# Group norm's inverse deviation: one power on Pool in place of ScalarE's square root and VectorE's reciprocal

## The chip, the cores and the metric

The kernel runs on one core of one Trainium2 chip. The metric is the device time of one execution in microseconds (us); lower is better. The engines of the core are named as the profile names them: PE is TensorE, DVE is VectorE, ACT is ScalarE, POOL is GpSimd, and SP issues the DMAs. Each works through its own list of instructions in order, and they wait for each other by semaphores.

## What is computed

Two layers run over a batch of 8, with 112 tokens of 512 channels each. The first is an RWKV-6 block: layer norm, five mixed inputs, a recurrence over the tokens for 32 heads of 16 channels, a group norm over each head, a gate, the output projection `Wo`, a second layer norm and a gated feed-forward part. The second layer lets its output attend to 375 context tokens, followed by an RMS norm and a feed-forward net. The part that the change touches is the group norm:

```python
y = outs.transpose(1, 0, 2, 3)                      # (B, L, H, S), S = 16
gm = jnp.mean(y, axis=-1, keepdims=True)
gv = jnp.mean((y - gm) ** 2, axis=-1, keepdims=True)
y = ((y - gm) * jax.lax.rsqrt(gv + EPS)).reshape(B, L, C) * gn_w + gn_b
x = x + y * g @ Wo.T
```

with `EPS = 1e-05`. Everything is float32.

## The kernel before

The kernel is written engine by engine, with every wait by hand; nothing is scheduled by a tool. Each engine has a function `turn(b, nxt, c)`. Turn `b` does the first layer of batch `b`, and beside it the attention of batch `c = b - 1`. There are 8 turns (the first has no attention beside it), and behind them the feed-forward net of all batches. The order of the calls within `turn` is the order of the engine's work.

Near the end of a turn the group norm stands between the recurrence and the projection. The values are laid out with 128 partitions and 4 x 112 columns; the variance has 128 partitions and 112 columns, one column for each token, and is repeated over the 4 groups of columns. The steps are:

- DVE, `group_norm`: L504 adds up y, PE takes the means (`head_means` into bank 5, L1031), L506 subtracts them, L508 squares, PE takes the variance (`head_means` into bank 6, L1031, semaphore `gvar`).
- ACT, L854: the square root of variance plus epsilon, from bank 6 into `sx[:, 0, :]`, 128x112 (semaphore `gsd`).
- DVE, L510: its reciprocal into `sx[:, 1, :]` (semaphore `grstd`), and L512 multiplies the centred values by it (semaphore `yn_ready`).
- ACT, L859, four times: weight and bias of the norm (semaphore `ya_ready`).
- DVE: from the second turn on, `rms_norm(c)` stands here (L587, L589, a wait for a power on Pool, L592). It belongs to the attention of the batch before. Then `gated` (L517) multiplies by the gate.
- PE, L972: the projection `Wo` (`to_rows` in `turn`). Ahead of it PE has `context(b, 4)` (L1004), which needs none of this, and behind it `context(b, 5)`.
- DVE: `channel_mix` adds the input (L523) and takes the layer norm's statistics (L427, L430, L432), Pool takes their power -0.5 (L361, 112 partitions x 1), L434 normalizes, and PE transposes.

Pool already takes powers: the helper `rstd` (L361) raises one number for each of 112 partitions to -0.5, with the exponent from the tile `neghalf` (128x1). Pool's other work in a turn is `mixed` (L374), `scan_input` (L381, L384) 16 times over 8 chunks of the recurrence's inputs, and a sum (L367).

ScalarE needs a table of functions loaded for a root, and another one for the exponentials and hyperbolic tangents. L847 is a dummy root of one number; it draws the load of the root's table ahead of the three `context` copies (L775) that stand before L854. The load of the other table is ahead of L874, the next tanh.

Of the kernel before, what the change touches and what calls it, by code (L numbers as in the profile page):

```python
# [21 lines left out]
ALU = mybir.AluOpType  # L22
ACT = mybir.ActivationFunctionType
AX = mybir.AxisListType

P = 128
B, T, C = 8, 112, 512
# [18 lines left out]
EPS_LN, EPS_RMS = 1e-5, 1e-6  # L46
# [13 lines left out]
def build(nc, a, out):  # L60
    with ExitStack() as ctx:
        address = {}

        def sb(name, shape, dt=F32):
            buf = ctx.enter_context(nc.sbuf_tensor(name, shape, dt))
            size = 4
            for n in shape[1:]:
                size *= n
            address[name] = nc.sbuf_base - size
            return buf  # L70
# [5 lines left out]
        def sem(name):  # L76
            return ctx.enter_context(nc.semaphore(name))
# [27 lines left out]
        neghalf = sb("neghalf", [P, 1])  # L105
        eps = sb("eps", [P, 1])
        table = sb("table", [1, 1])
# [10 lines left out]
        sx = sb("sx", [P, NT, T])  # L118
# [72 lines left out]
        bank = [ctx.enter_context(nc.psum_tensor(f"bank{i}", [P, 512], F32)) for i in range(8)]  # L191

        def tiles(i):
            return bank[i][:, 0:NT * T].rearrange("p (k t) -> p k t", k=NT)
# [15 lines left out]
        s = {n: sem(n) for n in names}  # L210
# [118 lines left out]
        @block.gpsimd  # L329
        def _(pool):  # L330
            g = nc.gpsimd
            g.memset(ident[:, :], 0.0).then_inc(s["init_pool"], 1)
            g.memset(head_mean[:, :], 0.0).then_inc(s["init_pool"], 1)
            g.memset(place[:, :], 1.0).then_inc(s["init_pool"], 1)
            g.memset(neghalf[:, :], -0.5).then_inc(s["init_pool"], 1)
            g.memset(eps[:, :], EPS_LN).then_inc(s["init_pool"], 1)
            g.memset(ws[:, :, 0:1], -MASKED).then_inc(s["init_pool"], 1)
            g.memset(ks[:, :, 0:1], 0.0).then_inc(s["init_pool"], 1)
            g.memset(vt[:, :, 0:1], 0.0).then_inc(s["init_pool"], 1)
            pool.wait_ge(s["init_pool"], 8)  # L340
            g.affine_select(out=ident[:, :], in_=ident[:, :], compare_op=ALU.not_equal, fill=1.0, base=0,
                            pattern=[[-1, P]], channel_multiplier=1).then_inc(s["init_pool"], 1)

            off = H - HT
            g.affine_select(out=place[:, :], in_=place[:, :], compare_op=ALU.is_ge, fill=0.0, base=S * off,
                            pattern=[[-S, 2 * H - HT]], channel_multiplier=1).then_inc(s["init_pool"], 1)
            pool.wait_ge(s["init_pool"], 10)
            g.affine_select(out=place[:, :], in_=place[:, :], compare_op=ALU.is_ge, fill=0.0, base=S - 1 - S * off,
                            pattern=[[S, 2 * H - HT]], channel_multiplier=-1).then_inc(s["init_pool"], 1)


            for j in range(2 * NT - 1):
                n = H * (j - NT + 1)
                g.affine_select(out=head_mean[:, :], in_=head_mean[:, :], compare_op=ALU.not_equal, fill=1.0 / S,
                                base=n, pattern=[[-1, P]], channel_multiplier=1).then_inc(s["init_pool"], 1)
                pool.wait_ge(s["init_pool"], 12 + j)

            def rstd(buf, due, done, b):

                pool.wait_ge(s[due], b + 1)  # L360
                g.tensor_tensor(buf[:, 1:2], buf[:, 0:1], neghalf[0:T, :], ALU.pow).then_inc(s[done], 1)  # L361

            def latents_and_bias(c):

                pool.wait_ge(s["lat_ready"], c + 1)
                pool.wait_ge(s["ob_ready"], 1)
                g.tensor_tensor(lat_ob[:, :], lat[:, :], ob_rows[:, :], ALU.add).then_inc(s["latob_ready"], 1)  # L367

            def mixed(b, j):

                pool.wait_ge(s["mix_ready"], b * NMIX + j + 1)
                if j >= 3:
                    pool.wait_ge(s[("pv_ready", "pk_ready")[j - 3]], b + 1)
                g.tensor_tensor(xj[:, j % 3], tmp[:, j % 2], xa[:, :, 1:T + 1], ALU.add).then_inc(s["xj_ready"], 1)  # L374

            def scan_input(b, i):

                k, half, buf = i // 2, i % 2, scan[i % NBUF]
                pool.wait_ge(s[f"vb_loaded{i % NBUF}"], b * 32 + 16 * (i // NBUF) + 16)
                pool.wait_ge(s["ks_ready"], b + 1)  # L380
                g.tensor_tensor(buf, buf, ks[:, k:k + 1, 0:T].broadcast_to([P, VS, T]), ALU.mult  # L381
                                ).then_inc(s["a_ready"], 1)
                pool.wait_ge(s["a_ready"], b * NCH + i + 1)
                g.tensor_tensor(buf[:, :, 0:1], buf[:, :, 0:1],  # L384
                                s0[:, k, bass.ds(b, 1), half * VS:(half + 1) * VS].rearrange("p b a -> p a b"),
                                ALU.add).then_inc(s["s0_put"], 1)

            def turn(b, nxt, c=None):
                for j in range(NMIX - 1):
                    mixed(b, j)  # L390
                scan_input(b, 0)
                mixed(b, NMIX - 1)
                for i in range(1, NCH):
                    if i == NBUF and c is not None:
                        latents_and_bias(c)
                    scan_input(b, i)
                if c is not None:
                    rstd(small_y, "ve3", "rstd3", c)
                rstd(small, "ve2", "rstd2", b)
                rstd(small, "ve1", "rstd1", nxt)  # L400

            rstd(small, "ve1", "rstd1", 0)
            turn(0, 1)
            with pool.Fori(1, B) as b:
                turn(b, pool.snap(b + 1), pool.snap(b - 1))
            latents_and_bias(B - 1)
            rstd(small_y, "ve3", "rstd3", B - 1)

            pool.wait_ge(s["w2_loaded"], 32)
            for b in range(B):  # L410
                pool.wait_ge(s[f"lat_back{b % BC}"], 16 * (b // BC + 1))
                g.tensor_tensor(lat_all[:, b % BC, :], lat_all[:, b % BC, :], b2_rows[:, :], ALU.add
                                ).then_inc(s["latb2_ready"], 1)
# [3 lines left out]
        def _(dve):  # L417
            v = nc.vector
# [80 lines left out]
            def group_norm(b):  # L499
                def per_head(ap):  # L500
                    return ap.unsqueeze(1).broadcast_to([P, NT, T])
                dve.wait_ge(s["y1_ready"], b + 1)
                dve.wait_ge(s["yacc_ready"], b * NT + NT)
                v.tensor_tensor(y_cols, tiles(7), ruk[:, :, :], ALU.add).then_inc(s["y_ready"], 1)  # L504
                dve.wait_ge(s["gmean"], b + 1)
                v.tensor_tensor(y_cen, y_cols, per_head(bank[5][:, 0:T]), ALU.subtract).then_inc(s["gcen"], 1)  # L506
                dve.wait_ge(s["gcen"], b + 1)
                v.tensor_tensor(y_sq, y_cen, y_cen, ALU.mult).then_inc(s["gsq"], 1)  # L508
                dve.wait_ge(s["gsd"], b + 1)
                v.reciprocal(sx[:, 1, :], sx[:, 0, :]).then_inc(s["grstd"], 1)  # L510
                dve.wait_ge(s["grstd"], b + 1)
                v.tensor_tensor(y_norm, y_cen, per_head(sx[:, 1, :]), ALU.mult).then_inc(s["yn_ready"], 1)  # L512

# [205 lines left out]
        def _(act):  # L719
            c_ = nc.scalar  # L720
# [50 lines left out]
            def context(b, n):  # L771
                act.wait_ge(s["ctx_ready"], b * 7 + n + 1)
                src = bank[CTX_BANK[n]]
                if n < NT:
                    c_.activation(kt[:, n, 0:NCTX], src[:, 0:NCTX], ACT.Identity,  # L775
                                  bias=V["k_b"][:, n:n + 1]).then_inc(s["ctx_kept"], 1)
                else:
                    c_.copy(vv[0:KT_ROWS, n - NT, :], src[0:KT_ROWS, :]).then_inc(s["ctx_kept"], 1)
# [26 lines left out]
            def turn(b, nxt, nxt_row, c=None):  # L805
# [38 lines left out]
                    keep_inverse(c)  # L844
                decays(b, 3)

                c_.activation(table[:, :], eps[0:1, :], ACT.Sqrt)  # L847

                context(b, 0)
                context(b, 1)  # L850
                context(b, 2)

                act.wait_ge(s["gvar"], b + 1)
                c_.activation(sx[:, 0, :], bank[6][:, 0:T], ACT.Sqrt, bias=eps[:, :]).then_inc(s["gsd"], 1)  # L854
                act.wait_ge(s["yn_ready"], b + 1)
                if c is None:
                    act.wait_ge(s["gnv_loaded"], 16 * 2 * NT * NT)
                for k in range(NT):
                    i = c_.activation(ruk[:, k, :], y_norm[:, k, :], ACT.Identity,  # L859
                                      bias=gnv[:, 1, k:k + 1], scale=gnv[:, 0, k:k + 1])  # L860
# [472 lines left out]
```

## Time and profile before

| | |
|---|---|
| time, median of 3 runs | 1222.49 us (1221.03 to 1231.17) |
| the profiled execution: its own time | 1224.26 us |
| its span (first to last instruction) | 1222.2 us |
| mean granted TensorE clock | 0.911 |
| PE busy | 1051.5 us, 86% of the span |
| DVE busy | 625.0 us, 51% |
| ACT busy | 411.2 us, 34% |
| POOL busy | 270.3 us, 22% |

A busy share is an average over stages that are limited by different things. PE is busiest, but its share says nothing on the stretch around the group norm; there one reads who waits for whom.

### The profile page before, as it was taken

The page shows a single profiled execution, that of the slowest core. Times are in us where ns is not written, and L with a number is a line of the kernel's source. Part 1 is how long each engine was busy: PE and PEld are TensorE (multiplying, and loading weights), DVE is VectorE, ACT ScalarE, POOL GpSimd, SP SyncE. Part 2 cuts the span into 40 slices and gives each one's busy share as a digit, 9 for nine tenths or more (in the row PEclk, how much of TensorE's full clock was granted, in tenths as well). Part 3 has the DMA queues.
Part 4 walks back from the last instruction along what each step waited for, and adds up shares of the span by engine and source line. Part 5 has one row for each costly group of instructions (what it writes and reads, how often), then busy time and mean ns, then how long its engine had stood idle before and what let it go on. Part 6 is the DMA issues. An engine that isn't in the chain of part 4 may idle for free.

```text
span 1222.2 us, 18100 instructions
## 1 busy us (share of the span) xinstructions
PE 1051.5 (86%) x6748; PEld 741.1 (61%) x6748; DVE 625.0 (51%) x1204; ACT 411.2 (34%) x934; POOL 270.3 (22%) x231
## 2 busy tenths in 40 slices
PE   5658998799789978997799879987998697999998
PEld 5525684368447834674477447843784364788886
DVE  2543248425952594358335842684268423644544
ACT  3112244134422442253235312442254225533332
POOL 2420143105410540144014400540053000200100
PEclk9768997899899989998899779998998895899999
DMA  7470122012201120122012201220122046000200
GB/s 286 117 225 8 33 69 67 1 48 68 66 8 40 68 66 15 33 68 66 15 33 68 66 10 38 68 66 8 40 68 66 0 182 232 1 0 0 61 0 30
DMA packets 25779, 73.23 MB, mean 60 GB/s; under 512 B 8173, under 2 KB 10093, under 8 KB 24350
## 3 DMA queue, kind: packets, MB, share of 16 engines
q1 hardware_dynamic: 25758, 72.94, 18.8%
q8 instruction: 14, 0.23, 0.1%
q14 instruction: 7, 0.06, 0.0%
HBM read 65.82 MB, written 7.11 MB: 60 GB/s over the span
## 4 chain that ended last, share of the span: by engine, by line
issue 41%; PE 31%; POOL 13%; DVE 7%; SPq 2%; DMA 2%; ACT 2%; POOLq 0%; DVEq 0%; ACTq 0%
POOL region L381 9%; PE bank L1241 7%; PE bank L1229 6%; PE bank L965 5%; DVE region L489 3%; PE bank L1000 3%; PE bank L972 3%; DMA region<-v_scratch 2%; PE bank L1031 2%; POOL region L384 2%; SPq L237 2%; PE bank L1015 1%; DVE region L496 1%; PE bank L1049 1%; POOL xj L374 1%
## 5 line engine op out<-in xcount | busy, mean ns | idle before, releaser
L965 PE MATMUL bank<-xj,wbig 128*128 128x112 f32 x1280 | 174.7, 302 | 29.2 <-DVE xj L533 23.8
L965 PEld LDWEIGHTS bank<-xj,wbig 128*128 128x128 f32 x1280 | 169.1, 217 | 34.2 <-DVE xj L533 25.5
L381 POOL TENSOR_TENSOR region<-region,ks 128x896 f32<-128x896 f32 x64 | 139.2, 2174 | 221.6 <-DMA region<-v_scratch 221.5
L457 DVE SCALAR_TENSOR_TENSOR tmp<-bank,vec,sx 128x112 f32<-128x112 f32 x160 | 41.7, 327 | 183.4 <-PE bank L987 181.3
L745 ACT ACTIVATE smb<-smb,nmax 112x487 f32<-112x487 f32 x128 | 88.1, 690 | 80.8 <-DVE nmax L569 80.8
L1049 PE MATMUL bank<-ident,smb 112*125 112x112 f32 (+1 forms) x512 | 88.1, 313 | 29.4 <-ACT smb L745 28.9
L496 DVE TENSOR_TENSOR region<-region,rt 128x896 f32<-128x896 f32 x64 | 105.4, 1647 | 7.4 <-ACT rt L833 1.8
L1000 PE MATMUL bank<-region,wbig 128*128 128x375 f32 x256 | 103.5, 559 | 0.0
L1015 PE MATMUL bank<-region,place 128*32 128x448 f32 x256 | 42.8, 751 | 68.7 <-DVE region L496 68.7
L1049 PEld LDWEIGHTS bank<-ident,smb 112*125 112x125 f32 (+1 forms) x512 | 66.0, 200 | 58.5 <-ACT smb L745 57.5
L569 DVE CUSTOM_DVE_ANT_0 smb<-bank,mask_b 112x487 f32<-112x487 f32 x128 | 78.1, 660 | 27.7 <-issue 27.7
L489 DVE TENSOR_TENSOR_SCAN region<-tmp,region 128x896 f32<-128x896 f32 x32 | 76.0, 2374 | 26.7 <-ACT tmp L801 19.0
L374 POOL TENSOR_TENSOR xj<-tmp,xa 128x448 f32<-128x448 f32 x40 | 42.0, 1058 | 214.8 <-DVE tmp L457 214.8
L1000 PEld LDWEIGHTS bank<-region,wbig 128*128 128x128 f32 x256 | 56.7, 229 | 49.7 <-issue 30.1
L1004 PE MATMUL bank<-wbig,region 128*125 128x512 f32 x192 | 86.5, 593 | 0.0
L489 DVE TENSOR_TENSOR_SCAN region<-xj,region 128x896 f32<-128x896 f32 x32 | 70.7, 2208 | 25.0 <-POOL region L384 24.4
L972 PE MATMUL bank<-wbig,lt 128*112 128x512 f32 x128 | 61.5, 625 | 0.0
L775 ACT ACTIVATE region<-bank,vec 128x375 f32<-128x375 f32 x32 | 18.2, 570 | 123.2 <-PE bank L1000 123.2
L753 ACT COPY pts<-bank 125x448 f32<-125x448 f32 x128 | 58.6, 533 | 2.8 <-PE bank L1049 2.4
L965 PE MATMUL bank<-lt,wbig 128*128 128x112 f32 x512 | 59.1, 276 | 0.0
L965 PEld LDWEIGHTS bank<-lt,wbig 128*128 128x128 f32 x512 | 57.9, 192 | 1.7 <-issue 1.7
L1004 PEld LDWEIGHTS bank<-wbig,region 128*125 128x125 f32 x192 | 34.8, 188 | 38.7 <-issue 38.7
(154 smaller groups left out, 1627.4 us busy)
## 6 DMA issues: line engine op xcount, KB each, us to landing
region<-v_scratch SPq DMA_DIRECT2D x64, 448.0 KB
wbig<-in_w SPq DMA_DIRECT2D x2, 4096.0 KB, 15.1
region<-in_ctxt SPq DMA_DIRECT2D x9, 750.0 KB, 4.6
wbig<-in_wbig SPq DMA_DIRECT2D x3, 2048.0 KB, 16.2
wbig<-in_wbig SPq DMA_DIRECT2D x3, 1024.0 KB
region<-in_wbig SPq DMA_DIRECT2D x2, 1024.0 KB, 10.9
x_in<-in_x SPq DMA_DIRECT2D x9, 224.0 KB, 2.6
v_scratch<-vt SPq DMA_DIRECT2D x32, 56.0 KB, 1.6
```

What stands on the lines that cost most here:

```text
L381: g.tensor_tensor(buf, buf, ks[:, k:k + 1, 0:T].broadcast_to([P, VS, T]), ALU.mult).then_inc(s["a_ready"], 1)
L489: v.tensor_tensor_scan(flat_buf, decay[c % 2], flat_buf, 0.0, ALU.mult, ALU.add).then_inc(s["s_ready"], 1)
L496: v.tensor_tensor(buf, buf, rt[:, c:c + 1, :].broadcast_to([P, VS, T]), ALU.mult).then_inc(s["prod_ready"], 1)
L569: v.tensor_tensor_reduce(sm[r], bank[r][0:T, 0:NKEY], mask_b[:, :], -1.0 / DH, 3e38, ALU.add, ALU.min, nmax[:, h:h + 1]).then_inc(s["maske ...
L745: c_.activation(sm[r], sm[r], ACT.Exp, bias=nmax[:, h:h + 1], scale=-1.0, accum_out=rsum[:, 0, h:h + 1]).then_inc(s["probs"], 1)
L965: i = t_.matmul(tiles(dst)[:, m, :], w[:, k, m * P:(m + 1) * P], x[:, k, :], start=k == 0, stop=k == NT - 1)
L972: i = t_.matmul(bank[dst][0:m, :], x[:, k, :], w[:, k, :], start=k == 0, stop=k == NT - 1)
L1000: i = t_.matmul(dst[:, 0:NCTX], W["kw"][:, k, n * P:(n + 1) * P], ctxt[:, k, :], start=k == 0, stop=k == NT - 1)
L1004: i = t_.matmul(dst[0:KT_ROWS, :], ctxt[:, k, r:r + KT_ROWS], W["vw"][:, k, :], start=k == 0, stop=k == NT - 1)
L1049: i = t_.transpose(tiles(r)[0:n, j, :], sm[r][:, j * KT_ROWS:j * KT_ROWS + n], ident[0:T, 0:T])
L1229: i = t_.matmul(bank[HID_BANK[p]][:, 0:BC * T], w[:, k, :], x[:, n * BC:(n + 1) * BC, k, :], start=k == 0 and w is wh and x is h1_hi, stop ...
L1241: i = t_.matmul(bank[OUT_BANK[b]][0:T, :], x[:, b * T:(b + 1) * T], w[:, :], start=start and x is xh and w is wh, stop=stop and x is xl)
```

## The change

On ACT the root (L854) and the dummy root that draws its table (L847) are taken out. On DVE the reciprocal (L510) gives way to an addition of epsilon that reads the variance from bank 6 and writes `sx[:, 0, :]`. On Pool a power of 128x112 numbers to -0.5 is added, from `sx[:, 0, :]` to `sx[:, 1, :]`. It stands behind the last `scan_input` and ahead of the helpers `rstd`. The multiplication L512 waits for it by the same semaphore as before.

```diff
@@ -394,6 +394,9 @@
                     if i == NBUF and c is not None:
                         latents_and_bias(c)
                     scan_input(b, i)
+                pool.wait_ge(s["gsd"], b + 1)
+                g.tensor_tensor(sx[:, 1, :], sx[:, 0, :], neghalf[:, :].broadcast_to([P, T]), ALU.pow
+                                ).then_inc(s["grstd"], 1)
                 if c is not None:
                     rstd(small_y, "ve3", "rstd3", c)
                 rstd(small, "ve2", "rstd2", b)
@@ -506,8 +509,8 @@
                 v.tensor_tensor(y_cen, y_cols, per_head(bank[5][:, 0:T]), ALU.subtract).then_inc(s["gcen"], 1)
                 dve.wait_ge(s["gcen"], b + 1)
                 v.tensor_tensor(y_sq, y_cen, y_cen, ALU.mult).then_inc(s["gsq"], 1)
-                dve.wait_ge(s["gsd"], b + 1)
-                v.reciprocal(sx[:, 1, :], sx[:, 0, :]).then_inc(s["grstd"], 1)
+                dve.wait_ge(s["gvar"], b + 1)
+                v.tensor_scalar(sx[:, 0, :], bank[6][:, 0:T], EPS_LN, None, ALU.add).then_inc(s["gsd"], 1)
                 dve.wait_ge(s["grstd"], b + 1)
                 v.tensor_tensor(y_norm, y_cen, per_head(sx[:, 1, :]), ALU.mult).then_inc(s["yn_ready"], 1)
 
@@ -844,14 +847,10 @@
                     keep_inverse(c)
                 decays(b, 3)
 
-                c_.activation(table[:, :], eps[0:1, :], ACT.Sqrt)
-
                 context(b, 0)
                 context(b, 1)
                 context(b, 2)
 
-                act.wait_ge(s["gvar"], b + 1)
-                c_.activation(sx[:, 0, :], bank[6][:, 0:T], ACT.Sqrt, bias=eps[:, :]).then_inc(s["gsd"], 1)
                 act.wait_ge(s["yn_ready"], b + 1)
                 if c is None:
                     act.wait_ge(s["gnv_loaded"], 16 * 2 * NT * NT)
```

The change adds three lines to the file, so the same instruction of DVE stands three lines lower in the changed kernel.

DVE's list in the loop over the turns, from the squares of the group norm on (`y`, `ysq` and `rows` hold its values, `xj` the normalized ones, `lat_ob` and `small_y` belong to the RMS norm of the batch before), before the change:

```order
L508 TENSOR_TENSOR rows<-ysq 128x448 [waits gcen]
L510 RECIPROCAL sx<-sx 128x112 [waits gsd]
L512 TENSOR_TENSOR xj<-ysq,sx 128x448 [waits grstd]
L587 TENSOR_TENSOR lat_ob<-bank,lat_ob 112x512 [waits latob_ready,op_ready]
L589 ISA rows_y,small_y<-lat_ob 112x512 [waits x1_ready]
L589 ISA small_y 112x1
L592 TENSOR_SCALAR rows_y<-lat_ob,small_y 112x512 [waits rstd3]
L517 SCALAR_TENSOR_TENSOR ruk<-ruk,gate 128x448 [waits ya_ready]
```

and with it:

```order
L511 TENSOR_TENSOR rows<-ysq 128x448 [waits gcen]
L513 TENSOR_SCALAR sx<-bank 128x112 [waits gvar]
L515 TENSOR_TENSOR xj<-ysq,sx 128x448 [waits grstd]
L590 TENSOR_TENSOR lat_ob<-bank,lat_ob 112x512 [waits latob_ready,op_ready]
L592 ISA rows_y,small_y<-lat_ob 112x512 [waits x1_ready]
L592 ISA small_y 112x1
L595 TENSOR_SCALAR rows_y<-lat_ob,small_y 112x512 [waits rstd3]
L520 SCALAR_TENSOR_TENSOR ruk<-ruk,gate 128x448 [waits ya_ready]
```

The reciprocal's place is taken by the addition, which waits for PE (`gvar`) and not for ACT. The multiplication waits for `grstd` as before, which now comes from Pool; nothing else moved.

Pool's list in the same loop, from the last chunk of the recurrence's inputs to the end of the turn, before the change:

```order
L381 TENSOR_TENSOR region<-region,ks 128x896 [waits ks_ready,vb_loaded3]
L383 REGISTER_ALU
L384 ISA [waits a_ready]
L384 TENSOR_TENSOR region<-region,s 128x8
L361 TENSOR_TENSOR small_y<-small_y,neghalf 112x1 [waits ve3]
```

and with it:

```order
L384 TENSOR_TENSOR region<-region,s 128x8
L398 TENSOR_TENSOR sx<-sx,neghalf 128x112 [waits gsd]
L361 TENSOR_TENSOR small_y<-small_y,neghalf 112x1 [waits ve3]
L361 TENSOR_TENSOR small<-small,neghalf 112x1 [waits ve2]
L360 REGISTER_ALU
L361 TENSOR_TENSOR small<-small,neghalf 112x1 [waits ve1]
```

The power of 128x112 stands alone between them, with the wait for DVE's addition.

## Rows read from the trace of the kernel before

**Rows 1.** The chain in time at the fourth group norm: start us, length us, what.
```profile
344.15 0.64 DVE y L504
344.79 0.04 issue
344.83 1.15 PE bank L1031 x8
...
349.44 0.36 ACT sx L854
349.80 0.02 issue
349.82 0.86 DVE sx L510
...
350.71 0.04 DVE xj L512
```

**Rows 2.** Timeline behind it: start, length us, engine, line, [idle before <-releaser].
```profile
349.24 3.61 PE L1004 MATMUL bank<-wbig,region 128*125 128x512 f32 x8
...
351.25 0.68 DVE L587 TENSOR_TENSOR lat_ob<-bank,lat_ob 112x512 f32<-112x512 f32 x1
351.37 1.60 ACT L859 ACTIVATE ruk<-xj,gnv 128x112 f32<-128x112 f32 x4 [1.58 <-DVE xj L512]
...
352.75 0.55 POOL L361 TENSOR_TENSOR small_y<-small_y,neghalf 112x1 f32<-112x1 f32 x1 [13.99 <-DVE small_y L589]
...
353.33 0.49 DVE L592 TENSOR_SCALAR rows_y<-lat_ob,small_y 112x512 f32<-112x512 f32 x1 [0.66 <-POOL small_y L361]
353.74 0.62 DVE L517 SCALAR_TENSOR_TENSOR ruk<-ruk,gate 128x448 f32<-128x448 f32 x1
...
354.41 3.69 PE L972 MATMUL bank<-wbig,ruk 128*112 128x512 f32 x8 [1.56 <-DVE ruk L517]
...
359.80 0.15 DVE L432 TENSOR_SCALAR small<-mv 112x1 f32<-112x1 f32 x1
360.04 0.55 POOL L361 TENSOR_TENSOR small<-small,neghalf 112x1 f32<-112x1 f32 x1 [6.74 <-DVE small L432]
...
360.62 0.55 DVE L434 TENSOR_SCALAR rows<-y,mv,small 112x512 f32<-112x512 f32 x1 [0.67 <-POOL small L361]
```

**Rows 3.** Root and reciprocal by line: duration min/median/max ns, first and last start us.
```profile
L854 ACT ACTIVATE sx<-bank,eps x8: 354/354/355, 98.9 to 961.5; 128x112 f32<-128x112 f32 x8
L510 DVE RECIPROCAL sx<-sx x8: 852/853/853, 99.3 to 961.9; 128x112 f32<-128x112 f32 x8
```

**Rows 4.** Pool's instructions by line, the same columns.
```profile
L361 POOL TENSOR_TENSOR small<-small,neghalf x17: 549/550/554, 5.4 to 986.5; 112x1 f32<-112x1 f32 x17
L384 POOL TENSOR_TENSOR region<-region,s x64: 209/835/1805, 42.0 to 947.5; 128x8 f32<-128x8 f32 x64
L374 POOL TENSOR_TENSOR xj<-tmp,xa x40: 1052/1057/1068, 20.2 to 903.0; 128x448 f32<-128x448 f32 x40
```

**Rows 5.** A sum of DVE that reads PSUM: line, xcount | busy us, mean ns | idle.
```profile
L457 DVE SCALAR_TENSOR_TENSOR tmp<-bank,vec,sx 128x112 f32<-128x112 f32 x160 | 41.7, 327 | 183.4 <-PE bank L987 181.3 <-POOL xj L374 2.1
```

**Rows 6.** ACT's timeline around the root's table, and the other table.
```profile
323.10 1.28 ACT L847 ACT_TABLE_LOAD   x1
324.40 0.20 ACT L847 ACTIVATE table<-eps 1x1 f32<-1x1 f32 x1
327.20 0.57 ACT L775 ACTIVATE region<-bank,vec 128x375 f32<-128x375 f32 x1 [2.60 <-PE bank L1000]
...
371.28 1.28 ACT L874 ACT_TABLE_LOAD   x1
...
374.15 0.60 ACT L874 ACTIVATE ysq<-bank 112x512 f32<-112x512 f32 x1 [1.59 <-PE bank L972]
```

**Rows 7.** PE's timeline at full clock and after a long wait: start, length us.
```profile
343.06 0.96 PE L1015 MATMUL bank<-region,place 128*32 128x448 f32 x8
...
452.88 1.72 PE L1015 MATMUL bank<-region,place 128*32 128x448 f32 x8 [4.20 <-DVE region L496]
454.52 5.39 PE L972 MATMUL bank<-wbig,lt 128*112 128x512 f32 x8
```

**Rows 8.** The stretch of rows 7: PE, PEld, DVE, ACT, POOL busy us, PEclk, DMA.
```profile
448.00:452.00 4.00, 0.68 (x3) 0.08 (x1) 3.90 (x2) 0.57 (x1) 2.08 (x1) 0.90 0.56 140
452.00:456.00 4.00, 3.12 (x10) 0.96 (x11) 3.71 (x3) 0.00 (x0) 3.50 (x2) 0.50 0.11 24
```

## The prediction

> **What bounds the kernel now.** PE is busiest over the whole span, but the change acts on one short place in each of 8 turns, so I read the chain of waits there first, in order of time [rows 1]. The reader is to see single steps of different engines, one after the other: DVE adds up y, PE takes the means, and at the end ACT's root (from 349.44), DVE's reciprocal (from 349.82) and the multiplication (from 350.71). From the start of the root to the start of the multiplication it is 350.71 - 349.44 = 1.27 us. By line, root and reciprocal take 354 to 355 and 852 to 853 ns in all 8 turns [rows 3], so this piece is the same in each.
>
> Then the timeline behind it, to see whether a change of those 1.27 us reaches PE [rows 2]. PE covers the start with context work that needs none of this, 3.61 us from 349.24, that is until 352.85. It then waits 1.56 us for the gate (L517) before it starts the projection at 354.41. L517 itself comes last in a row of DVE's work: the RMS norm of the other batch stands ahead of it, starts as soon as the multiplication lets it (L587 at 351.25, 0.54 us after the multiplication began), waits for a power on Pool and ends with L592. ACT's four scalings, the other thing L517 needs, end at 351.37 + 1.60 = 352.97, 0.77 us before L517 starts. So whatever moves the multiplication moves RMS norm, gate and projection by the same amount, and behind the projection DVE, Pool and PE follow one another again (L432, L361, L434). A delay passes through in full. A gain passes through as far as PE's 1.56 us of waiting reach.
>
> **The change part by part.**
>
> ACT loses the dummy root and its table load, 0.20 and 1.28 us in each turn, and since no root is left in the loop, the load of the other table ahead of L874 should go too. Both are covered: the root's table is ready 2.60 us of waiting before the next copy (L775), and the other load ends at 372.56 while ACT then still waits 1.59 us for PE's product [rows 6]. I cost both at nothing. If neither had a cover they would be 8 x (0.20 + 2 x 1.28) = 22 us. The skill bears on this, apart from the sum: the Trainium skill, ScalarE: Activation LUTs, on what a table load costs, gives about 2.7 us for one with its drain and puts exponential and root into different sets. By that an estimate for the 16 loads is 43 us if they were all on the path; this trace has 1.28 us for one and shows the cover.
>
> DVE loses 0.85 us of reciprocal and gets one addition from PSUM over 128x112. The trace has no such instruction. From below it is bounded by the 0.15 us of L432, which does the same on one column [rows 2], from above by the 0.33 us of L457, which has the same shape, also reads PSUM and does more [rows 5]. I take 0.33, the row with the same shape. ACT's root (0.35) is gone with its two handovers.
>
> Pool gets the power of 128x112. It isn't late by Pool's queue: Pool had waited 13.99 us before L361 at 352.75 [rows 2], and the powers behind the new one are asked for only after the multiplication. The handovers are read at L432, L361 and L434: 360.04 - (359.80 + 0.15) = 0.09 us into Pool and 360.62 - (360.04 + 0.55) = 0.03 us out of it. So with D for the new power's length, the multiplication starts 0.33 + 0.09 + D + 0.03 = D + 0.45 us after the variance is there, in place of 1.27. The turn becomes longer by **D - 0.82 us**, and D = 0.82 is the break-even.
>
> Everything hangs on D, which the trace doesn't show. Pool's rows [rows 4]: multiplications and sums take 1057 ns for 448 columns and at best 209 ns for 8, thus (1057 - 209) / 440 = 1.93 ns for a column and 209 - 8 x 1.93 = 194 ns for an instruction. The power of a single column takes 550 ns, and always the same to 5 ns. So one column of power costs 550 - 194 = 356 ns, some 180 times a column of multiplication. What isn't known is how much of that is repeated for each further column.
>
> - Lower end: nothing is repeated but the plain rate, D = 0.550 + 111 x 0.00193 = 0.76 us. Even a power as cheap as a multiplication would be 0.194 + 112 x 0.00193 = 0.41 us.
> - Upper end: all of it is repeated, D = 0.194 + 112 x 0.356 = 40.1 us.
>
> I take 45 ns for each further column, an eighth of the 356. This is a choice between ends far apart, and it lies nearer in ratio to the power's own row (a factor of 8) than to the multiplication's (a factor of 23), because that is the one row with this operation: a column of it takes hundreds of ns of dependent work, of which a loop over columns can overlap a part, but hardly all. D = 0.550 + 111 x 0.045 = 5.5 us, and the turn grows by 5.5 - 0.82 = 4.7 us.
>
> Then PE: its wait ahead of the projection grows from 1.56 to 6.3 us. The trace shows what follows a wait of that kind. After 4.20 us of waiting PE's granted clock is 0.50 of full speed, so 1.2 GHz in place of 2.4 [rows 8], and the next two groups take 1.72 in place of 0.96 us and 5.39 in place of 3.69 us [rows 7, 2]: 2.5 us lost. The projection is of the very shape of the second group. After 1.56 us of waiting it ran at its full rate. I take 2.0 us for each turn, between nothing and 2.5.
>
> Sum: 8 x (4.7 + 2.0) = 54 us. The profiled execution took 1224.3 us around a span of 1222.2; that gives 1278, and since it lay 1.8 us above the median of the runs shown, the forecast is **1276 us**.
>
> **The rivals.**
>
> *The power streams like a multiplication* (the other side: no slower). Place: the one Pool instruction. Price: D = 0.76 us is 0.06 under break-even, so -0.5 us in all, and in the very best case (0.41 us and an addition of 0.15) 8 x (0.41 - 1.00) = -4.7 us. It decides from the cost of a further column: up to 16 ns (D = 2.35 us, 8 x 1.53 = 12 us) the time stays within 1%. For it: the multiplication keeps 194 ns of start-up from being repeated, and if the 356 ns are mostly the start-up or the drain of a long pipeline, they are paid once too; that the single power's time is so constant fits this. Against it: such a power would need to be as fast per column as a product of two numbers. Time: 1218 to 1235, about 1222. The Trainium skill, GPSIMD Engine Reference, on elementwise work side by side with VectorE, gives this rule: about 2.6 cycles per element and core for an operation with two inputs, set by the reads of its operands and not by the arithmetic. Applied to the power, that rule gives this rival. The trace agrees with its rate for a multiplication (1.93 ns), but shows 356 ns for one column of power.
>
> *Nothing overlaps.* Each column pays the 356 ns anew: D = 40.1 us, the turn grows by 39.3 and by up to 2.5 for the clock, 8 x 41.8 = 334 us, time about 1556. For it: the single power is the only measured one, and a routine that is called once for each column would do just this. Against it: the multiplication overlaps nearly everything.
>
> *The removed ACT work was on the path after all.* Then up to 22 us would come back, and with a power at its lower end the time would be 1200. ACT's waits of 2.60 and 1.59 us behind the loads speak against it, in this turn as in the others, since the durations repeat.
>
> **How the numbers follow.** Part overlap (a further column at 16 to 120 ns, time 1235 to 1347; the upper end is D = 0.55 + 13.3 = 13.9 us, 8 x (13.1 + 2.5) = 125 us): 0.43. Power streams: 0.27. Nothing overlaps: 0.26. ACT's work on the path: 0.02. Something not seen: 0.02. The time is that of the likeliest, 1276, with its own range 1235 to 1347. The range that should hold 8 in 10 has to take in both the streaming and the serial case, for leaving out the serial one would already leave out more than 2 in 10: 1218 to 1560. A measurement of this kernel can tell a change from none from about 1% on. From the cases: faster by over 1% 0.02, within 1% 0.27, slower by over 1% 0.71.
>
> **What would show it.** In the changed kernel's profile: the length of the new Pool power (5.5 us here; 0.8 and 40 for the rivals), with the same length in all 8 turns; DVE's multiplication waiting for Pool by just that; the addition at 0.33 us or less; PE's wait for L517's successor at 6.3 us and the projection behind it longer than 3.69 us; no table load in the loop and no shift of the copies behind it. I am wrong if the span doesn't change by 8 x (D - 0.82) plus the clock's part. That would mean that a piece of the chain had slack that I didn't see, or that the turns absorb the delay elsewhere, for instance in waits for DMA that need no longer be waited for.

## The result

| | before | changed |
|---|---|---|
| time, median of the runs | 1226.83 us (4 runs) | 1388.81 us (4 runs, 1369.5 to 1393.57) |
| ratio | | 1.124, 95% interval 1.112 to 1.137 |
| the profiled execution: time, span | 1224.26, 1222.2 us | 1369.5, 1367.4 us |
| mean granted TensorE clock | 0.911 | 0.873 |
| PE, DVE, ACT, POOL busy | 1051.5, 625.0, 411.2, 270.3 us | 1058.7, 621.7, 386.1, 415.1 us |

The ratio, here and in the experiments, leaves out the runs in a slower state that the chip is in at times, so it is lower than the quotient of the medians (1.132 here).

The kernel became slower by an eighth. The profile says at once where to look: Pool's busy time grew by 144.8 us, and the span by 145.2. (That the two are so nearly equal is chance, as the account of the waits below shows.) The page's groups of the changed kernel (line, engine, operation, out<-in, count | busy us, mean ns | idle before it and who ended it) show the new power, and the two instructions that wait for it, the multiplication directly and the projection further down the chain:

```profile
L398 POOL TENSOR_TENSOR sx<-sx,neghalf 128x112 f32<-128x112 f32 x8 | 145.8, 18229 | 99.8 <-DVE sx L513 99.8
L971 PE MATMUL bank<-wbig,ruk 128*112 128x512 f32 x64 | 46.1, 886 | 150.4 <-DVE ruk L520 150.4
L515 DVE TENSOR_TENSOR xj<-ysq,sx 128x448 f32<-128x448 f32 x8 | 5.0, 625 | 146.7 <-POOL sx L398 146.7
```

One power of 128x112 takes 18.2 us. By line (duration min/median/max in ns, first and last start) it is the same in every turn, and the addition ahead of it is short:

```profile
L398 POOL TENSOR_TENSOR sx<-sx,neghalf x8: 18222/18231/18232, 101.3 to 1089.2; 128x112 f32<-128x112 f32 x8
L513 DVE TENSOR_SCALAR sx<-bank x8: 273/274/275, 100.9 to 1088.8; 128x112 f32<-128x112 f32 x8
```

The chain of waits at the fourth group norm (start, length us, what), which answers to [rows 1]. From the addition's start to the multiplication's it is now 397.87 - 379.25 = 18.62 us, where it had been 1.27:

```profile
378.33 0.89 PE bank L1030 x8
379.23 0.02 issue
379.25 0.29 DVE sx L513
379.54 0.07 issue
379.60 18.24 POOL sx L398
397.85 0.02 issue
397.87 0.03 DVE xj L515
```

And the timeline behind it, which answers to [rows 2]. The order is the old one, shifted, except that the projection takes longer: 6.15 us in place of 3.69.

```profile
397.87 0.62 DVE L515 TENSOR_TENSOR xj<-ysq,sx 128x448 f32<-128x448 f32 x1 [18.34 <-POOL sx L398]
398.41 0.68 DVE L590 TENSOR_TENSOR lat_ob<-bank,lat_ob 112x512 f32<-112x512 f32 x1
...
400.89 0.62 DVE L520 SCALAR_TENSOR_TENSOR ruk<-ruk,gate 128x448 f32<-128x448 f32 x1
...
401.57 6.15 PE L971 MATMUL bank<-wbig,ruk 128*112 128x512 f32 x8 [18.91 <-DVE ruk L520]
...
414.85 3.83 PE L964 MATMUL bank<-xj,wbig 128*128 128x112 f32 x32 [2.92 <-DVE xj L536]
```

The clock's column explains the projection. These are stretches of the same place (PE, PEld, DVE, ACT, POOL busy us, PEclk, DMA share, GB/s): PE stands still for 18.9 us, its granted clock falls to 0.50, which is the level of 1.2 GHz, and rises again while the projection runs.

```profile
383.00:398.00 15.00, 0.00 (x0) 0.00 (x0) 0.13 (x1) 0.00 (x0) 14.84 (x1) 0.60 0.00 0
398.00:401.50 3.50, 0.00 (x0) 0.00 (x0) 2.80 (x6) 2.62 (x7) 0.55 (x1) 0.50 0.00 0
401.50:408.00 6.50, 6.43 (x10) 2.57 (x11) 0.25 (x2) 0.00 (x0) 0.00 (x0) 0.61 0.00 0
411.00:419.00 8.00, 5.08 (x43) 4.61 (x42) 2.68 (x9) 3.21 (x10) 0.00 (x0) 1.00 0.19 57
```

Who waited for whom, over all turns, balances the account. The first three are the changed kernel's, in us in total, times, longest:

```profile
PE bank L971 <- DVE ruk L520: 150.4, 8, 18.9
...
DVE y L526 <- PE bank L971: 46.8, 8, 6.4
...
DVE tmp L543 <- ACT tmp L871: 36.2, 8, 5.1
```

and these are the same waits in the kernel before:

```profile
DVE tmp L540 <- ACT tmp L872: 43.4, 8, 6.6
...
DVE y L523 <- PE bank L972: 30.2, 8, 3.8
...
PE bank L972 <- DVE ruk L517: 11.8, 8, 1.6
```

PE waits 150.4 - 11.8 = 138.6 us more for the gate, which is 8 x (18.62 - 1.27) = 138.8. DVE waits 46.8 - 30.2 = 16.6 us more for the slower projection. And 43.4 - 36.2 = 7.2 us come back: behind the second layer norm, PE's products (L965 before, L964 now) took 5.45 us before in this turn and take 3.83 now. The line of before:

```profile
365.23 5.45 PE L965 MATMUL bank<-xj,wbig 128*128 128x112 f32 x32 [2.93 <-DVE xj L533]
```

This differs from turn to turn. In the kernel before the eight groups take 6.72, 5.36, 5.45, 5.45, 3.83, 6.93, 5.38 and 6.84 us, in the changed kernel 5.45, 3.83, 3.83, 5.45, 5.46, 5.45, 5.45 and 3.83: 46.0 us in all and 38.8. The sum of the three waits is 148.0 us against 145.2 of span; the remaining 2.8 aren't assigned.

### The profile page after: what moved, and what is told of

It is laid out like the page before. It is cut to its first block, busy times and chain, and to the rows that moved or that the text cites. A ratio compares the mean times of both kernels' runs of the same rounds, so it can differ in the third digit from the quotient of the medians.

```text
span 1367.4 us, 18076 instructions
## 1 busy us (share of the span) xinstructions
PE 1058.7 (77%) x6748; PEld 739.0 (54%) x6748; DVE 621.7 (45%) x1204; ACT 386.1 (28%) x902; POOL 415.1 (30%) x239
## 4 chain that ended last, share of the span: by engine, by line
issue 37%; PE 28%; POOL 22%; DVE 6%; SPq 2%; DMA 2%; ACT 1%; POOLq 0%; DVEq 0%; ACTq 0%
POOL sx L398 11%; POOL region L381 8%; PE bank L1240 6%; PE bank L1228 6%; PE bank L964 5%; PE bank L971 3%; PE bank L999 3%; DVE region L492 3%; DMA region<-v_scratch 2%; PE bank L1030 2%; POOL region L384 2%; SPq L237 1%; PE bank L1048 1%; PE bank L1014 1%; DVE region L499 1%
## 5 line engine op out<-in xcount | busy, mean ns | idle before, releaser
L381 POOL TENSOR_TENSOR region<-region,ks 128x896 f32<-128x896 f32 x64 | 136.2, 2129 | 221.3 <-DMA region<-v_scratch 221.1
L964 PE MATMUL bank<-xj,wbig 128*128 128x112 f32 x1280 | 164.5, 291 | 30.1 <-DVE xj L536 23.8
L964 PEld LDWEIGHTS bank<-xj,wbig 128*128 128x128 f32 x1280 | 158.8, 206 | 35.1 <-DVE xj L536 25.5
L398 POOL TENSOR_TENSOR sx<-sx,neghalf 128x112 f32<-128x112 f32 x8 | 145.8, 18229 | 99.8 <-DVE sx L513 99.8
L971 PE MATMUL bank<-wbig,ruk 128*112 128x512 f32 x64 | 46.1, 886 | 150.4 <-DVE ruk L520 150.4
L971 PEld LDWEIGHTS bank<-wbig,ruk 128*112 128x112 f32 x64 | 16.4, 272 | 180.0 <-DVE ruk L520 157.1
L858 ACT ACTIVATE ruk<-xj,gnv 128x112 f32<-128x112 f32 x32 | 12.8, 470 | 235.6 <-DVE xj L515 235.6
L515 DVE TENSOR_TENSOR xj<-ysq,sx 128x448 f32<-128x448 f32 x8 | 5.0, 625 | 146.7 <-POOL sx L398 146.7
```

The costliest lines, as they stand in the source:

```text
L398: g.tensor_tensor(sx[:, 1, :], sx[:, 0, :], neghalf[:, :].broadcast_to([P, T]), ALU.pow).then_inc(s["grstd"], 1)
L964: i = t_.matmul(tiles(dst)[:, m, :], w[:, k, m * P:(m + 1) * P], x[:, k, :], start=k == 0, stop=k == NT - 1)
L971: i = t_.matmul(bank[dst][0:m, :], x[:, k, :], w[:, k, :], start=k == 0, stop=k == NT - 1)
```

## The experiments

Each kernel was timed beside the kernel before on the same chip, so the ratio is the number to compare.

**e1: what a power costs by its columns.** The kernel before, with this at the end of Pool's last turn (`pw` is a new scratch tile of 128x144, `pw_done` a semaphore that lets each instruction wait for the one ahead):

```diff
             latents_and_bias(B - 1)
+            g.memset(pw[:, 0:56], 0.7).then_inc(s["pw_done"], 1)
+            g.memset(pw[:, 112:144], -0.5).then_inc(s["pw_done"], 1)
+            done = 2
+            half = neghalf[:, :]
+            for out_, in_, by, op in (
+                    [(pw[:, 56:56 + n], pw[:, 0:n], half.broadcast_to([P, n]), ALU.pow) for n in (1, 2, 4, 8, 16, 32, 56)]
+                    + [(pw[:, 56:56 + n], pw[:, 0:n], half.broadcast_to([P, n]), ALU.mult) for n in (1, 8, 56)]
+                    + [(pw[0:16, 56:88], pw[0:16, 0:32], neghalf[0:16, :].broadcast_to([16, 32]), ALU.pow),
+                       (pw[:, 56:88], pw[:, 0:32], pw[:, 112:144], ALU.pow)]):
+                pool.wait_ge(s["pw_done"], done)
+                g.tensor_tensor(out_, in_, by, op).then_inc(s["pw_done"], 1)
+                done += 1
```

> The kernel before, with twelve more Pool instructions on scratch numbers (all 0.7) at the end of the last turn, where Pool had 60 us of waiting: powers of 128 partitions by 1, 2, 4, 8, 16, 32 and 56 columns, multiplications of 1, 8 and 56, a power of 16 partitions by 32, and one of 128 by 32 with the exponent read from a full tile. They are there for their lengths alone. The changed kernel shows one column at 0.54 us and 112 at 18.23. Theory 'every column costs the same, and about 380 ns are paid once': 0.38 + 0.16 n, so 0.7 for 2, 1.0 for 4, 1.66 for 8, 2.9 for 16, 5.5 for 32, 9.3 for 56, and the same 5.5 for 16 partitions and for the full exponent tile. Rival 'columns are worked on in groups': steps, the same length for 1, 2 and 4 columns, say. Rival 'it depends on the numbers': equal numbers give another line than the group norm's variances, 9.3 for 56 no longer fits. The multiplication of one column should be about 0.2 us, of 56 about 0.3.

Pool's groups of this kernel, by shape (count | busy us, mean ns | idle before). Where the count is 2, a power and a multiplication of the same shape stand together:

```profile
L418 POOL TENSOR_TENSOR pw<-pw,neghalf 128x56 f32<-128x56 f32 x2 | 9.5, 4768 | 0.2
L418 POOL TENSOR_TENSOR pw<-pw 128x32 f32<-128x32 f32 x1 | 5.4, 5427 | 0.1
L418 POOL TENSOR_TENSOR pw<-pw,neghalf 128x32 f32<-128x32 f32 x1 | 5.4, 5414 | 0.1
L418 POOL TENSOR_TENSOR pw<-pw,neghalf 16x32 f32<-16x32 f32 x1 | 5.4, 5404 | 0.1
L418 POOL TENSOR_TENSOR pw<-pw,neghalf 128x16 f32<-128x16 f32 x1 | 2.9, 2894 | 0.1
...
L418 POOL TENSOR_TENSOR pw<-pw,neghalf 128x4 f32<-128x4 f32 x1 | 1.0, 1012 | 0.1
L418 POOL TENSOR_TENSOR pw<-pw,neghalf 128x2 f32<-128x2 f32 x1 | 0.9, 926 | 0.1
L418 POOL TENSOR_TENSOR pw<-pw,neghalf 128x1 f32<-128x1 f32 x2 | 0.9, 431 | 0.2
```

and by line, where the minimum is the multiplication of one column and the maximum the power of 56:

```profile
L418 POOL TENSOR_TENSOR pw<-pw,neghalf x11: 190/1012/9258, 978.8 to 1002.0; 128x1 f32<-128x1 f32 x2, 128x8 f32<-128x8 f32 x2, 128x56 f32<-128x56 f32 x2, 128x2 f32<-128x2 f32 x1
```

From 16 to 32 columns a power grows by (5414 - 2894) / 16 = 158 ns for a column, from 32 to 56 by (9258 - 5414) / 24 = 160, and from there to the changed kernel's 112 by (18231 - 9258) / 56 = 160. It is a straight line with 0.3 to 0.4 us paid once; below 4 columns the points lie above it by up to 0.3 us (926 ns for 2 columns; the power of one column took 2 x 431 - 190 = 672 ns, where L361 takes 549). The multiplication of 56 columns took 2 x 4768 - 9258 = 278 ns. Sixteen partitions cost as much as 128, an exponent from a full tile as much as a repeated one, and equal numbers (all 0.7) lie on the line of the real variances. So from 4 columns on there are no steps by groups of columns, and these two sets of numbers make no difference.

**e2: the same change with a cheap Pool instruction.** The changed kernel with this edit. It leaves out the power, so the group norm is scaled by other numbers; only its time is of use:

```diff
-                g.tensor_tensor(sx[:, 1, :], sx[:, 0, :], neghalf[:, :].broadcast_to([P, T]), ALU.pow
+                g.tensor_tensor(sx[:, 1, :], sx[:, 0, :], neghalf[:, :].broadcast_to([P, T]), ALU.mult
```

> The changed kernel with a multiplication in place of the new power, so that the group norm is scaled by a wrong number; all else stays. It sets the length D of the Pool instruction to about 0.4 us with the whole rest of the change. Theory 'only D matters': the addition measured 0.27, so the multiplication starts 0.27 + 0.09 + 0.4 + 0.03 = 0.8 us after the variance in place of 1.27, so 8 x 0.5 = 4 us less than before, about 1219 to 1221, ratio 0.997, and a projection at its full rate. Rival 'the removed ACT work or the reordered waits cost something by themselves': another time than that, above before or far under it (up to 22 us less).

Ratio 0.997, interval 0.993 to 1.001 (median 1215.4 us against 1220.5). In its timeline the multiplication starts 344.93 - 344.17 = 0.76 us after the addition, and the projection runs at 3.69 us:

```profile
344.17 0.28 DVE L513 TENSOR_SCALAR sx<-bank 128x112 f32<-128x112 f32 x1 [4.14 <-PE bank L1030]
344.52 0.37 POOL L398 TENSOR_TENSOR sx<-sx,neghalf 128x112 f32<-128x112 f32 x1 [12.94 <-DVE sx L513]
344.93 0.62 DVE L515 TENSOR_TENSOR xj<-ysq,sx 128x448 f32<-128x448 f32 x1 [0.49 <-POOL sx L398]
```

8 x (0.76 - 1.27) = -4.1 us was to be expected, -5.1 is the difference of the medians, which the interval can't tell from nothing. All the rest of the change, the two table loads and the reciprocal taken away and the new wait, is thus worth at most some 5 us either way. The loss comes from the power's length and what follows from it.

**e3: half of the columns.** The power on the first 56 of the 112 columns; the other half of the deviations isn't computed:

```diff
-                g.tensor_tensor(sx[:, 1, :], sx[:, 0, :], neghalf[:, :].broadcast_to([P, T]), ALU.pow
+                g.tensor_tensor(sx[:, 1, 0:T // 2], sx[:, 0, 0:T // 2], neghalf[:, :].broadcast_to([P, T // 2]), ALU.pow
```

> The changed kernel with the power on the first 56 of the 112 columns; the other half of the deviations is left uncomputed. Theory 'cost per column, passed through in full': D = 0.38 + 56 x 0.16 = 9.3 us, so the turn is 9.3 + 0.39 - 1.27 = 8.4 us longer than before, 67 us, and about 9 us for the clock net of what comes back later, 76 us or a ratio of 1.062. Rival 'a part is absorbed elsewhere in the turn': the time is not on the straight line between e2 and the changed kernel.

Ratio 1.073, interval 1.066 to 1.080, median 1307.2 us. The power takes 9.28 us:

```profile
L398 POOL TENSOR_TENSOR sx<-sx,neghalf 128x56 f32<-128x56 f32 x8 | 74.3, 9284 | 105.7 <-DVE sx L513 105.7
```

From e2 to e3 the power grows by 8.91 us and the time by 91.8, which is 8 x 8.91 = 71.3 and 20.5 more. The larger part of those is the clock: DVE's wait for the projection is 50.1 us here and 30.2 in e2, as before the change, while its later wait (L543) falls from 40.6 to 34.1, so 19.9 - 6.5 = 13.4 us net. The other 7 us aren't assigned; medians of two kernels are compared here. From e3 to the changed kernel (e8 below, by its ratio 1.119 about 1366 on this chip) it is 8 x 8.95 = 71.6 us of power against some 59 measured, with an interval of about 20 us to either side. The clock's part isn't proportional to the wait: the projection's loss has its full size at a wait of 10 us already (50.1 us, where the changed kernel has 46.8). I had put it at 9 us net and the whole ratio at 1.062, which the measured interval excludes; the power's own length passes through in full, within these intervals.

**e4: the table loads back in.** The dummy root stands again ahead of ACT's `context` copies:

```diff
+                c_.activation(table[:, :], eps[0:1, :], ACT.Sqrt)
```

> The changed kernel with the dummy root put back on ACT, so that both table loads of each turn are back (16 x 1.28 us of ACT). Theory 'the loads were covered': the same time as the changed kernel, 1.12 of before, within its scatter. Rival 'they were on the path': up to 22 us more than it, 1.14.

Ratio 1.119, interval 1.108 to 1.129, the changed kernel's own within the scatter, and 8 loads of this table and 8 of the other are in its trace again. It excludes neither 1 nor 5 us, but a cost of 22 us, which would be 1.14, is excluded.

```profile
361.81 1.28 ACT L850 ACT_TABLE_LOAD   x1
363.11 0.20 ACT L850 ACTIVATE table<-eps 1x1 f32<-1x1 f32 x1
370.33 0.57 ACT L778 ACTIVATE region<-bank,vec 128x375 f32<-128x375 f32 x1 [7.03 <-PE bank L1001]
```

After the load ACT still waits 7.03 us for PE. The load lies in its idle time. This cover is longer than the 2.60 us that the kernel before has there [rows 6]; that the loads cost nothing in that kernel too rests on e2, which is without them and no faster than its shorter chain accounts for.

**e5 and e7: PE kept busy through the wait.** To see whether the lower clock costs anything in the end, PE gets products in the wait whose result is overwritten. e5 has twenty of them written out, e7 four in a loop of five rounds:

```diff
                 context(b, 4)
+                with pe.Fori(0, 5):
+                    for k in range(NT):
+                        t_.matmul(bank[5][0:T, :], W["Wk"][:, k, 0:T], W["Wk"][:, k, :],
+                                  start=k == 0, stop=k == NT - 1)
                 pe.wait_ge(s["yg_ready"], b + 1)
```

> The changed kernel, with 20 matrix products of the projection's size (five times 4, of a weight by itself, into a bank that the projection overwrites) on PE between the context work and the wait for the gate, about 18 us of work in a wait of 19 us; the result is not used. Theory 'the long wait lowers PE's clock, and that costs 2.1 us a turn in the projection': the projection is back at 3.69 us in place of up to 7.2, DVE's wait for it back at 3.8 us, and the time falls by up to 17 us against the changed kernel, less whatever stood gained further on (PE's products after the second layer norm were faster in the changed kernel than before), ratio about 1.11 against before. Rival 'the clock costs nothing in the end': the same time as the changed kernel.

e5 came out at 1.156, interval 1.148 to 1.163, slower than the change itself, although the projection was back at its full rate (DVE's wait for it 30.2 us). PE's waits show a new one, for nothing that the profile names, and the page's DMA part shows what moved at that time:

```profile
PE bank L964 <- issue: 35.8, 7, 5.7
```

```profile
q8 instruction: 69, 1.13, 0.3%
```

The queue that brings instructions moved 69 packets and 1.13 MB, where it moved 14 and 0.23 MB in the kernel before. The seven waits are at the start of the seven rounds of PE's loop over the turns, and behind the third of them the products took 9.49 us where they take 7.40 in the changed kernel: PE's granted clock is 0.50 in their first 4.2 us. e7 takes the written-out instructions away and keeps the work.

> As e5, but the 20 products are 4 products in a loop of five turns, so that PE's list of instructions grows by 8 matrix instructions and their weight loads and not by 40. In e5 PE's projection was back at its full rate, but PE waited 36 us more for nothing that the profile shows at the start of the loop over the turns, and the instruction queue moved 1.13 MB in place of 0.23. Theory 'e5's loop had outgrown what PE holds, and had to be fetched again in each turn': the queue is back near 0.23 MB and the waits are gone, and what is left shows the clock: up to 17 us less than the changed kernel (e8), less about 7 us that had come back further on, ratio 1.11 to 1.12 against 1.125. Rival 'the filling itself costs': still near 1.15.

> The changed kernel again, as it is, so that e7 has it beside it on the same chip: 1.12 to 1.13 of before, its power at 18.2 us.

In e7 the instruction queue is back at 14 packets and 0.23 MB and the seven waits are gone, as the theory on e5 said. The time is 1.127, interval 1.119 to 1.135 (median 1377.4 us), above the 1.11 to 1.12 expected, and the changed kernel beside it (e8) 1.119, interval 1.105 to 1.134 (1380.8 us). So no gain is seen from keeping PE busy. One of clearly over 1% is excluded; the 10 us that I expected net lie just at the edge of that. Its trace shows what stands against the faster projection:

```profile
402.68 3.69 PE L971 MATMUL bank<-wbig,ruk 128*112 128x512 f32 x8 [1.74 <-DVE ruk L520]
...
413.50 6.85 PE L964 MATMUL bank<-xj,wbig 128*128 128x112 f32 x32 [2.93 <-DVE xj L536]
```

and the clock in these two stretches (columns as above, PEclk third from the end):

```profile
402.60:406.40 3.80, 3.72 (x9) 1.71 (x10) 0.03 (x1) 0.00 (x0) 0.00 (x0) 1.00 0.00 0
...
413.50:420.40 6.90, 6.90 (x33) 6.86 (x34) 0.92 (x4) 0.02 (x1) 0.00 (x0) 0.54 0.22 67
```

The projection is fast, at a granted clock of 1.00, and the products behind the second layer norm, ahead of which PE waits 2.9 us in this turn in every version, are slow instead, at 0.54: 6.85 us, where the changed kernel has 3.83 and the kernel before 5.45. DVE's later wait in e7 (answering to the 36.2 above) is 48.9 us. Of the 16.6 us that the warm projection saves, 12.7 are lost again there in this execution.

How much is lost there varies. e5's projection is as warm, and its later wait is 43.2 us, like the 43.4 of the kernel before. Turn by turn the traces with a cold projection (the changed kernel, e3, e4, e8) show one pattern: in the ten turns from the second on whose projection took 5.96 us or more, these products ran at full rate (3.83 us for a whole group), and in all turns whose projection took 5.87 us or less they took 5.45. PE's wait ahead of the projection was the same 18.9 us in both kinds within the changed kernel. So the length of that wait doesn't decide it; what goes with fast products is a projection that had lost more. No run tests whether the one causes the other. e3's first turn (6.55 us and then 6.57) doesn't fit.

**e6: the RMS norm ahead of the reciprocal.** The prediction read that in the kernel before the gate waits 0.77 us longer for DVE's own order than for ACT. This is a test of that reading, and a version that might beat both. `rms_norm` is split in its first two instructions (`rms_sum`) and its last (`rms_rows`):

```diff
                 v.tensor_tensor(y_sq, y_cen, y_cen, ALU.mult).then_inc(s["gsq"], 1)
+                if c is not None:
+                    rms_sum(c)
                 dve.wait_ge(s["gsd"], b + 1)
...
-                group_norm(b)
+                group_norm(b, c)
                 if c is not None:
-                    rms_norm(c)
+                    rms_rows(c)
                 gated(b)
```

> The kernel before, with ScalarE's root and the reciprocal kept, and the first two instructions of the RMS norm on DVE moved ahead of the reciprocal, into the 2.5 us in which DVE waits for variance and root; its last instruction stays behind the multiplication. Theory 'DVE's order makes the gate wait 0.77 us longer than ACT's four scalings': the gate starts about 0.7 us earlier in each of 7 turns, 5 us less in all, ratio 0.996. Rival 'that time is covered': no change. If the RMS norm's sum or its power delayed the reciprocal, slower by as much.

Ratio 0.993, interval 0.988 to 0.997 (median 1217.9 us against 1224.7). The gate now starts 353.68 - 351.39 = 2.29 us after the multiplication, where it had been 353.74 - 350.71 = 3.03 [rows 1, 2], and it waits for ACT:

```profile
351.39 0.62 DVE L514 TENSOR_TENSOR xj<-ysq,sx 128x448 f32<-128x448 f32 x1
351.94 0.48 DVE L596 TENSOR_SCALAR rows_y<-lat_ob,small_y 112x512 f32<-112x512 f32 x1
352.06 1.59 ACT L864 ACTIVATE ruk<-xj,gnv 128x112 f32<-128x112 f32 x4 [1.58 <-DVE xj L514]
...
353.68 0.63 DVE L519 SCALAR_TENSOR_TENSOR ruk<-ruk,gate 128x448 f32<-128x448 f32 x1 [1.26 <-ACT ruk L864]
```

The gate's start is the same 2.29 us after the multiplication in every turn of the trace, and PE's wait ahead of the projection is 0.83 us where it was 1.56. 7 x 0.74 = 5.2 us, or 0.4%, was expected; the interval of the measured 0.7% holds it. By that interval this is a version slightly faster than both kernels.

## Why the prediction was wrong

Slower was forecast, and slower it was, but by 12% and not by 4%. The step that failed is one number: "I take 45 ns for each further column, an eighth of the 356".

- **The cost of a further column.** e1 shows 158 to 160 ns for each. Of the 356 ns by which the single power exceeds a multiplication, not an eighth is repeated but nearly a half. The power is then 18.2 us long and not 5.5, and that is 8 x 12.7 = 102 of the 113 us between 1276 and 1389. With 159 ns in the prediction's own sum it reads D = 0.55 + 111 x 0.159 = 18.2 us, 8 x (18.2 - 0.82 + 2.0) = 155 us, and 1377 us. Beside the profiled executions, which grew by 145.2 us, the corrected sum is 10 us too large, and 7.2 of those are the gain behind the second layer norm.
- **How it was chosen.** The ends were right (0.76 and 40.1 us), the choice between them had nothing behind it, and the two cases beside it left out what happened: partial overlap was said to be 16 to 120 ns, no overlap 356, and nothing lay between. The wide range held the time, the likeliest case's own range (1235 to 1347) didn't. Nothing in the rows could set this price, so the gap between 120 and 356 ns should have been a case of its own. That the direction came out right rests on both cases in which further columns cost something, not on the 45 ns. (For the bound of 16 ns the formula gives D = 2.33 us and not 2.35, which changes nothing.)
- **The formula D - 0.82** was right. The addition took 0.27 and not 0.33 us. In the changed kernel the multiplication starts 18.62 us after the addition's start with D = 18.23, thus D + 0.39, and the turn grows by D - 0.88. e2 confirms it at the other end: 0.76 us with D = 0.37.
- **A delay passes through in full**: PE's wait grew by 138.6 us against 138.8 from the chain. Nothing in the turn absorbs it.
- **The clock.** 2.0 us a turn were forecast for the projection; it is 16.6 / 8 = 2.1. That a gain behind the second layer norm (7.2 us in this pair of profiles) stands against it wasn't seen. The turns compared under e7 show that the two go together: where the projection lost most, the products behind lost nothing. Its size varies: DVE's wait there is 40.6 to 43.4 us in the three profiles with a short wait ahead of the projection (before, e2, e6), and 34.1 to 41.1 in the four with a long one (e3, the changed kernel, e8, e4).
- **ACT's table loads and root were put at nothing.** e4 and e2 bear it out, with 22 us excluded and a few us left open. The rival that had them on the path is out.
- **The rule of the Trainium skill, GPSIMD Engine Reference, on elementwise work** (some 2.6 cycles per element for an operation with two inputs) was measured there on an addition, and the page names the reads of the two inputs as its floor. A floor says nothing on how much dearer another operation is, and the prediction's rival read it as a price. In order of size it fits the multiplication here: (278 - 190) / 55 = 1.6 ns a column in e1. The power costs 160 ns a column. The other page, the Trainium skill, ScalarE: Activation LUTs, on what the engine computes, advises VectorE's reciprocal followed by a square root on ScalarE for this quantity, on grounds of accuracy. The kernel before takes the same two steps in the other order, and here they are also the shorter way, 1.27 us against 18.6.

## What to carry to other kernels

Before an operation is moved to an engine on which only its one-column form was ever seen, measure it at its new size: add it on scratch data where that engine is idle, and the profile gives its price by column in one run at no cost to the rest. A short instruction that is fine as a helper for 112 single numbers is not so for 112 columns of them. And what lies in idle time, like the two table loads here, is no gain, while a chain that several engines walk one after the other passes each microsecond on.

## What the runs showed of the hardware

- Pool's power costs 158 to 160 ns for each column and 0.3 to 0.4 us once, from 4 columns to 112, on 16 partitions as on 128 (5404 and 5414 ns for 32 columns), with the exponent repeated or from a full tile (5414 and 5427 ns). A multiplication beside it costs under 2 ns a column.
- With a loop body of PE that had grown by 40 matrix instructions and their weight loads, the instruction queue moved 1.13 MB in place of 0.23, which fits the body being brought in again in each round, and each round began with a wait of about 5 us that the profile puts down to nothing. The same work as an inner loop had neither. At what size of the body this begins wasn't tried.
- The clock that PE is granted can be lost in a place where nothing was changed: with PE busy ahead of the projection, the products 11 us later took 6.85 us in e7, at the place where they took 3.83 in the changed kernel. Over the eight turns it was 51.4 us in e7, 46.0 in the kernel before and 38.8 in the changed one. After the same wait of 18.9 us they took 3.83 us behind a projection of 5.96 to 6.35 us and 5.45 behind one of 5.19 to 5.87. What sets how much of the loss falls into the projection is open.
